# The MLP's token layer norm two groups ahead in a window-attention, MLP and channel-attention kernel: GpSimd's queue for the last slices, joins ahead of gathers

## What is computed

```python
# first block: shifted-window attention and an MLP over tokens (C = 96)
xn = layernorm(x)                                # over channels
x  = shortcut + unshift(window_attention(shift(xn)))
h  = layernorm(x, norm2_g, norm2_b)              # the token layer norm of the MLP
x  = x + (gelu(h @ fc1_w + fc1_b) @ fc2_w + fc2_b)
# second block: channel attention
xn = (x - mean) * rsqrt(var + 1e-5) * ln_g + ln_b     # mean, var over a whole image
Q, K, V = three times: 1x1 grouped convolution, then depthwise 3x3 convolution of xn
attn = softmax(K^T Q / alpha)                    # 8 heads, 12x12
out  = w_f @ (V attn) + b_f + xn
```

## Time and profile before

| | us |
|---|---|
| median of three runs | 526.51 |
| lowest and highest run | 522.05, 529.94 |
| the profiled execution | 523.45 |
| its span on the core | 521.8 |

### The profile page before, as it was taken

The page is one execution under the profiler, slowest core; times in us unless marked ns, Lnnn a source line. Parts: engine busy times, 40 slices in busy tenths (PEclk is TensorE's granted clock), DMA queues, the critical chain, the costliest instruction groups (busy, mean ns, idle before and its releaser), DMA issues.

```text
span 521.8 us, 23235 instructions
## 1 busy us (share of the span) xinstructions
PE 501.1 (96%) x8942; PEld 321.5 (62%) x8942; DVE 367.0 (70%) x1001; ACT 304.6 (58%) x763; POOL 183.0 (35%) x233
## 2 busy tenths in 40 slices
PE   7999999999999999998899999976999999999996
PEld 7777777777777777776565334333555565555553
DVE  2599999999999999998603466624665655656544
ACT  2477778877777887776434667611344444444332
POOL 8544344344434434442460202222223323323300
PEclk8899999999999999999999999995799999999998
DMA  4211101111110111100031142575244444344411
GB/s 80 62 34 31 30 22 44 30 31 31 31 28 22 26 30 30 30 2 3 12 96 33 37 99 63 118 130 138 66 111 119 109 116 115 109 117 115 111 45 31
DMA packets 41175, 32.47 MB, mean 62 GB/s; under 512 B 19240, under 2 KB 36776, under 8 KB 41128
## 3 DMA queue, kind: packets, MB, share of 16 engines
q1 hardware_dynamic: 37544, 26.11, 19.9%
q0 software_dynamic: 3584, 5.72, 5.1%
HBM read 18.36 MB, written 7.13 MB: 49 GB/s over the span
## 4 chain that ended last, share of the span: by engine, by line
PE 43%; DVE 2%; DMA 2%; SPq 2%; issue 1%; ACT 0%; DVEq 0%
PE ps_hidden L1626 18%; PE ps_hidden L1161 6%; PE ps_y L1661 4%; PE ps_y L1172 4%; PE ps_y L1667 4%; PE ps_turn L1642 3%; PE ps_turn L1652 2%; DMA padded_x<-x_pad 1%; PE ps_y L110 1%; SPq L1108 1%; DMA stream<-y_sliced 1%; SPq L1046 1%; PE ps_turn L909 1%; PE ps_turn L916 1%; DVE normed L1327 0%
## 5 line engine op out<-in xcount | busy, mean ns | idle before, releaser
L413 POOL TENSOR_TENSOR scores<-scores,peak 128x768 f32<-128x768 f32 x64 | 94.3, 1474 | 129.9 <-DVE peak L582 129.9
L1626 PE MATMUL ps_hidden<-x_stack,conv_w 40*32 40x256 f32 x3072 | 101.8, 392 | 0.3 <-issue 0.3
L1046 POOL DMA_DIRECT2D x_stack<-padded_x x96 | 52.4, 548 | 127.9 <-PE ps_hidden L1626 77.6
L476 ACT COPY probs_t<-ps_probs 128x768 f32<-128x768 f32 x64 | 51.1, 799 | 40.1 <-PE ps_probs L736 40.1
L1626 PEld LDWEIGHTS ps_hidden<-x_stack,conv_w 40*32 40x32 f32 x3072 | 53.6, 108 | 30.5 <-issue 15.9
L574 DVE TENSOR_TENSOR scores<-ps_scores,bias 128x768 f32<-128x768 f32 x64 | 61.3, 958 | 6.1 <-PE ps_scores L726 4.4
L582 DVE TENSOR_REDUCE peak<-scores 128x12 f32<-128x768 f32 x64 | 61.0, 953 | 2.4
L749 PE MATMUL ps_out<-v_blocks,probs_t 128*64 128x54 f32 x1536 | 57.2, 224 | 1.0 <-ACT out_t L481 0.9
L749 PEld LDWEIGHTS ps_out<-v_blocks,probs_t 128*64 128x64 f32 x1536 | 50.2, 138 | 12.3 <-issue 12.2
L470 ACT ACTIVATE scores<-scores 128x768 f32<-128x768 f32 x64 | 54.2, 847 | 1.5 <-POOL scores L413 1.5
L736 PE MATMUL ps_probs<-ident,scores 128*128 128x128 f32 x384 | 54.3, 277 | 0.0
(11 more groups left out here) (157 smaller groups left out, 831.1 us busy)
## 6 DMA issues: line engine op xcount, KB each, us to landing
x_stack<-padded_x SPq DMA_DIRECT2D x96, 54.0 KB
x_stack<-padded_x POOLq DMA_DIRECT2D x96, 54.0 KB, 2.7
padded_x<-x_pad SPq DMA_DIRECT2D x32, 121.5 KB, 2.5
x_sliced<-stream SPq DMA_DIRECT2D x48, 64.0 KB, 2.0
stream<-y_sliced SPq DMA_DIRECT2D x48, 64.0 KB, 2.1
out<-y_sb SPq DMA_DIRECT2D x32, 96.0 KB, 2.0
x_now<-in_x SPq DMA_DIRECT2D x32, 72.0 KB, 1.8
stream<-in_x SPq DMA_DIRECT2D x32, 72.0 KB, 1.9
```

The source lines that it names most:

```text
L413: nc.gpsimd.tensor_tensor(sc, sc, peak[:, par, p, :].unsqueeze(2).to_broadcast((128, HEADS, WN)), ALU.subtract).then_inc(s["shifted"], 1)
L476: nc.scalar.copy(probs_t[:, :], ps_turned).then_inc(s["turned_copied"], 1)
L1046: engine.dma_start(last.x_stack[64 * half + i * HC:64 * half + (i + 1) * HC, slot, :, :], rows).then_inc(landed[slot], 16)
L1626: mm = nc.tensor.matmul(ps[32 * k:32 * k + 32, r, :], conv_w[rows, kind, j, k, :], grid(x_stack[rows, slot, k, :], PADW)[:, :, j:j + W], s ...
```

## The change

- TensorE turns the tokens of group g+2 during group g (`ahead`), so those of group 2 in group 0 and those of group 3 in group 1; group 2 turns none. In group 0 the first two fills shrink from 15 to 9 matmuls; both turns of chunks 0 and 1 come ahead of the fill. At the end of the first stage 9 more matmuls of a zero constant are issued behind the last slice's transposes.
- ScalarE copies the tokens accordingly, and makes the deviation of group g+2 after the third GELU of group g, where before it came after the second.
- VectorE measures chunks 8 to 11 before it copies `normed` of group 1, and 12 to 15 among the residuals of group 0.
- The slices of group 3 are issued by GpSimd, on its own semaphore, after its scaling and before its gathers. On SP, `join_y(2, 0)` stands ahead of the gathers of images 0 and 1, and `join_y(2, 2)` ahead of the gathers of images 2 and 3.
- `take_moments(2, 0, 4)` becomes `take_moments(2, 0, 8)`, and `measure_images` of step 0 goes.

```diff
+        fill(nc, ps_out[0:C, 0, 0:C], blank[:, :], 9)          # behind turn_first_slice, end of stage 1
...
+    def slice_x(engine, g, landed):
+
+        need(engine, s["mixed_ready"], (g - 1) * SLICES * 2)
+        for c in range(SLICES):
+            for r in range(QUARTERS):
+                at = (g * QUARTERS + r) * CHUNK
+                engine.dma_start(x_sliced[32 * r:32 * r + 32, g % 2, c, :],
+                                 stream[32 * c:32 * c + 32, at:at + CHUNK]).then_inc(landed, 16)
...
-        for g in range(GROUPS - 2):
-            for c in range(SLICES):
-                join_y(g, c)
-            sp.wait_ge(x_in[g % 2], (g // 2 + 1) * PARTS)
-            slice_x(g + 2)
-        join_y(GROUPS - 2, 0)
+        for c in range(SLICES):
+            join_y(0, c)
+        sp.wait_ge(x_in[0], PARTS)
+        slice_x(sp, 2, x_in[0])
+        for c in range(SLICES):
+            join_y(1, c)
         write_padded(sp, last, 0, 0)
         write_padded(sp, last, 1, 1)
+        join_y(2, 0)
         gather_taps(sp, last, 0, 0, 0, 0, last.stacked_sp)
         gather_taps(sp, last, 1, 0, 1, 0, last.stacked_sp)
-        join_y(GROUPS - 2, 1)
+        join_y(2, 1)
         write_padded(sp, last, 2, 2)
         write_padded(sp, last, 3, 3)
+        join_y(2, 2)
         gather_taps(sp, last, 2, 0, 2, 0, last.stacked_sp)
         gather_taps(sp, last, 3, 0, 3, 0, last.stacked_sp)
-        join_y(GROUPS - 2, 2)
...
 # TensorE
-            if g > 1 and r < 2:
-                pe.wait_ge(s["normed_ready"], g * SLICES)
-            if g > 1 and r > 1:
+            if r < 2:
+                pe.wait_ge(s["normed_ready"], (g - 1) * SLICES)
+            else:
                 pe.wait_ge(s["tokens_copied"], k - 1)
...
+            if g + 1 < GROUPS and c < 2:                        # in turn_back
+                pe.wait_ge(s["tokens_copied"], (g + 1) * QUARTERS + 3 + c)
...
             up(g, 0)
+            if ahead:
+                turn_tokens((g + 2) * QUARTERS)
             if g == 0:
-                fill(nc, ps_y[0:C, 0, 0:C], average[:, :], 15)
-            if later:
-                turn_tokens((g + 1) * QUARTERS)
+                turn_tokens((g + 2) * QUARTERS + 1)
+                fill(nc, ps_y[0:C, 0, 0:C], average[:, :], 9)
...
             up(g, 1)
+            if ahead:
+                turn_tokens((g + 2) * QUARTERS + 2)
+                turn_tokens((g + 2) * QUARTERS + 3)
             if g == 0:
-                fill(nc, ps_y[0:C, 0, 0:C], average[:, :], 15)
+                fill(nc, ps_y[0:C, 0, 0:C], average[:, :], 9)
...
 # GpSimd
+        slice_x(pool, GROUPS - 1, x_in_last)
         for t in range(SLOTS):
             gather_taps(pool, last, t, 0, t, 1, last.stacked_pool)
...
 # ScalarE
             gelu(g, 2)
+            if ahead:
+                nc.scalar.preload_act_table_set("natural_log_exp_and_others")
+                token_deviation(nc, act, m, s, g + 2)
+                nc.scalar.preload_act_table_set("gelu_and_others")
...
 # VectorE
+        for k in range(2 * QUARTERS, 3 * QUARTERS):
+            measure(k)
         for c in range(SLICES):
             copy_normed(1, c)
...
-        take_moments(2, 0, 4)
+        take_moments(2, 0, 8)
...
-            for early in range(SLOTS - 1):
+            for early in range(1, SLOTS - 1):
```

More of the change, by code:

```diff
@@ L1082, in mlp @@
     x_in = [sem("x_in0"), sem("x_in1")]
+    x_in_last = sem("x_in_last")
     y_out = last.joined
@@ L1091, in tokens_home @@
         return by_blocks(ps_turn[:, k % 2, :])
-    def run_sp(sp):
-        def slice_x(g):
-            need(sp, s["mixed_ready"], (g - 1) * SLICES * 2)
-            for c in range(SLICES):
[L1098 to L1101, removed]
+    def slice_x(engine, g, landed):
[5 more added lines that the diff above has]
+                                 stream[32 * c:32 * c + 32, at:at + CHUNK]).then_inc(landed, 16)
+    def run_sp(sp):
         def join_y(g, c):
@@ L1109, in join_y @@
                              y_sliced[32 * r:32 * r + 32, g % 2, c, :]).then_inc(y_out[g % 2], 16)
-        slice_x(0)
-        slice_x(1)
+        slice_x(sp, 0, x_in[0])
+        slice_x(sp, 1, x_in[1])
         for half in range(ROUNDS):
@@ L1134, in run_sp @@
         for c in range(SLICES):
-            join_y(GROUPS - 1, c)
+            join_y(3, c)
     def run_pe(pe):
@@ L1184, in run_pe @@
             more = g + 1 < GROUPS
-            later = more and g > 0
+            ahead = g + 2 < GROUPS
             up(g, 0)
+            if ahead:
+                turn_tokens((g + 2) * QUARTERS)
             if g == 0:
-                fill(nc, ps_y[0:C, 0, 0:C], average[:, :], 15)
-            if later:
-                turn_tokens((g + 1) * QUARTERS)
+                turn_tokens((g + 2) * QUARTERS + 1)
+                fill(nc, ps_y[0:C, 0, 0:C], average[:, :], 9)
             if not more:
@@ L1198, in run_pe @@
                 down(g - 1, 0)
-            if later:
-                turn_tokens((g + 1) * QUARTERS + 1)
+            if ahead and g > 0:
+                turn_tokens((g + 2) * QUARTERS + 1)
             up(g, 1)
+            if ahead:
+                turn_tokens((g + 2) * QUARTERS + 2)
+                turn_tokens((g + 2) * QUARTERS + 3)
             if g == 0:
-                fill(nc, ps_y[0:C, 0, 0:C], average[:, :], 15)
-            if later:
-                turn_tokens((g + 1) * QUARTERS + 2)
-                turn_tokens((g + 1) * QUARTERS + 3)
+                fill(nc, ps_y[0:C, 0, 0:C], average[:, :], 9)
             if g > 0:
@@ L1284, in run_act @@
         for g in range(GROUPS):
-            later = 0 < g < GROUPS - 1
+            ahead = g + 2 < GROUPS
             gelu(g, 0)
-            if later:
+            if ahead:
                 for r in range(2):
-                    copy_tokens(nc, act, m, s, (g + 1) * QUARTERS + r, tokens_home(r))
+                    copy_tokens(nc, act, m, s, (g + 2) * QUARTERS + r, tokens_home(r))
             if g + 1 == GROUPS:
@@ L1334, in add_residual @@
             dve.wait_ge(s["y_ready"], n + 1)
-            dve.wait_ge(x_in[par], (g // 2 + 1) * PARTS)
+            if g + 1 < GROUPS:
+                dve.wait_ge(x_in[par], (g // 2 + 1) * PARTS)
+            else:
+                dve.wait_ge(x_in_last, PARTS)
             need(dve, y_out[par], g // 2 * PARTS)
@@ L1360, in run_dve @@
         nc.vector.tensor_scalar(w["taps_b"][:, 1:2], w["taps_b"][:, 1:2], last.recip_alpha[:, 0:1], None, ALU.mult).then_inc(last.taps_scaled, 1)
+        for k in range(2 * QUARTERS, 3 * QUARTERS):
+            measure(k)
         for c in range(SLICES):
             copy_normed(1, c)
-        measure(2 * QUARTERS)
-        measure(2 * QUARTERS + 1)
+        measure(3 * QUARTERS)
         add_residual(0, 0)
-        measure(2 * QUARTERS + 2)
-        measure(2 * QUARTERS + 3)
+        measure(3 * QUARTERS + 1)
+        measure(3 * QUARTERS + 2)
+        measure(3 * QUARTERS + 3)
         add_residual(0, 1)
```

5 lines of the change are left out of this document (removed).

## The result

The changed kernel takes 506.43 us (median of four runs, 504.95 to 508.78) against 524.28 for the kernel before (four runs, 520.97 to 529.94). The ratio is 0.9684, with a 95% interval of 0.9602 to 0.9766: faster by 3.2%, some 12 to 21 us. The ratios here leave disturbed executions out, so they can differ from the quotient of two medians. The profiled execution took 504.95, with a span of 503.3 us.

What follows compares the result with a forecast made beforehand. TensorE, busy 96% of the span, was taken as the bound, losing time to pauses and half clock. Savings 2.9 + 6.86 + 6.32 = 16.1 us from a 526.5 median gave 510.4, rounded to 510, range 504 to 519.

Steps and rivals of the forecast that it cites:

- (1): Barrier before the MLP: opens 0.9 us later, but the clock holds and the first up saves 1.76; net -0.9 us.
- (2): MLP, group 0: smaller fills plus turned chunks stay covered by GELU; two places give -0.26 us, bounds 0 and -0.4.
- (3): MLP, group 2: no tokens turned, up and down back to back, GELU still hides; net -1.77 us.
- (5): MLP to channel attention: joins issued earlier, so TensorE's pause (6.86 us) and the half clock behind it (6.32 us) go.
- group 3's joins: SP's queue: they end at about 348 us instead of 359.4, and step 1's measure_images finds them landed.
- The rule on GpSimd's descriptors: GpSimd's slices: the skill gives some 3100 ns per DMA beside a VectorE copy; twelve would take some 37 us.
- (A): Transition does not close: TensorE still stands 1.5 to 2 us and the clock falls; saved 7.8, time 518.7; chance 0.2.
- (B): GpSimd's slices held up by VectorE, decisive from 1.4 us an issue; time 530; chance 0.05.
- (C): Transition: joins not the true wait, another transfer holds it; only the MLP's 2.9 us saved, 523.6; chance 0.07.

Runs made afterwards that it cites:

- experiment 3: Kernel after without the 9 added matmuls at the barrier ending the first stage: 506.38 us (eight runs).
- experiment 1: Kernel before with only group 3's slices on GpSimd, joins ahead of gathers and eight moments at the end of the MLP: 507.3 us, ratio 0.9737.
- experiment 5: Kernel after with the slices of group 3 back on SP, behind the joins of group 1: 515.09 us, ratio 0.9853.
- experiment 11: Kernel after with 8 more VectorE statistics into a spare tile (2.7 us) ahead of the copy of image 0's tokens: 513.76 us, ratio 0.9872.
- experiment 6: Kernel after with SP's order around group 2 as before, joins behind gathers; slices stay on GpSimd: 515.04 us, ratio 0.9854.
- experiment 4: Kernel before with 36 constant matmuls in TensorE's pause ahead of image 0's 12x12 products: 516.62 us, ratio 0.9868.
- experiment 9: Kernel after with 5 matmuls at the barrier, 3 behind group 0's third up part, and two last-image pauses of stage 1 filled: 504.98 us, ratio 0.9694.
- experiment 7: Kernel after with four images' moments at the end of the MLP and the other four in step 0, as before: 509.6 us, ratio 0.9777.
- experiment 8: Kernel after with 5 matmuls in place of 9 at the barrier and 3 in place of 6 behind group 0's third up part: 505.6 us, ratio 0.9723.
- experiment 12: Kernel before with slices on GpSimd, joins ahead of gathers, eight moments, and stage 1's two last-image pauses filled: 509.16 us, ratio 0.9762.

## Why the prediction was right, point by point

The forecast was 510 us in 504 to 519, from 16.1 us saved; 506.43 was measured, and 17.85 us between the medians. Of the distance of 4.0 us to the unrounded 510.4, 2.2 lie in the kernel before, which was measured at 524.28 in place of 526.51. The mechanism was right. By its steps:

- **(1), the barrier**, net -0.9: in the profiles +0.77 for the later barrier and -1.76 for the clock, -0.99. Right here, but the argument was too sure: experiment 3 and six profiles show that the clock falls there only about half the time. In the mean this step is worth nothing by that count, so that it came out at -0.99 is luck, and leaving it out costs nothing.
- **(2), group 0**: `up` parts 5.39 us apart (255.66 to 261.05), as named (5.4). ScalarE's table loads fitted before the next GELU.
- **(3), group 2**: `up` and `down` back to back, GELU still hidden; the MLP is shorter by 3.91 - 1.76 = 2.15 us besides the clock, and 2.03 were forecast for (2) and (3). 0.14 of it is there without the layer norm part (experiment 1: 84.55 against 86.45 - 1.76).
- **(5), the transition**: the last join of group 2 issued at the moment its data were there and no wait on VectorE, as forecast; the pause went by 5.82 in place of 6.86. The missing 1.0 is the short stall of 0.50 us, and slower matmuls round it, inside image 1's first convolution. The clock stayed: 6.60 against 6.32, because the first of the two steps is 4.62 us and not 4.90. VectorE finished the copy at 342.34 and TensorE took it up at 344.11: 1.8 us to spare, 0.7 were forecast. The surplus is that stall with the slower matmuls round it.
- What the prediction had wrong in (5), though it didn't show in the time, is why slices had to leave SP. It argued with the joins of group 2. Experiment 5 shows that these would land in time anyway; it is group 3's joins, wanted in step 1 by `measure_images`, that need SP free. The prediction had them down in one sentence as harmless.
- **The rule on GpSimd's descriptors.** Twelve issues took 5.98 us (496 to 586 ns each) while VectorE was busy with residuals and normalisation. "SBUF — State Buffer" of the Trainium skill, as cited in the prediction, has some 3100 ns for one beside a copy by VectorE; nothing of that kind was seen with the operations that ran here: by its estimate twelve would have taken 37 us, and those of this tile landed 2.0 to 3.0 us after their issue. The kernel had no SBUF-to-SBUF copy by VectorE in that stretch, so the rule itself was not tested.
- **Rivals.** (A) did not come, but experiment 11 shows it 1.8 us of spare time away and prices a pause of 1.05 us at 5.3 us by stretches, 7.3 by medians. (B) did not come: 0.5 us an issue, where 1.4 were needed. (C) falls with experiments 1 and 6: the joins were the true wait.

The 3.5 us of the first stage in the two profiles are a difference of executions, not of kernels; the median's 17.85 us and its interval cover both 15.0 and 16.1, so no term can be corrected by it.

## What to carry to other kernels

A pause of about a microsecond on TensorE is priced by what its clock does behind it, mostly four to nine microseconds here, so look for the wait that ends it in the queue that issues the transfers, and set transfers with late readers behind those with early ones. When one queue is loaded, ask for every transfer left on it, not for the first late one alone: two joins and two readers stood here, and each half of the remedy alone gave half. When the runs of a kernel lie in heaps, find the short pauses ahead of the stretch where the clock differs, and fill them with constants in a bank that is free; compare traces by stretches, since a median over heaps hides parts of 2 us.

## What the runs showed that was not expected

- **The length of a pause of about one microsecond does not decide whether the clock falls.** Behind 0.93 and 0.62 us, with 0.91 us of work between, it fell in four of eleven profiles; behind 1.41 us in three of six; behind 1.05, 1.31, 1.35 and 0.76 with 0.44 us it fell; behind 0.50, 0.61, 0.92 and 1.47 it held. Behind 0.66 us it held in eight of eight. A fall cost 4.8 us once and 6.4 three times at the last image of the first stage, 1.76 us at the barrier, and in channel attention from 1.6 us (experiment 4) over 4.5 (experiment 11) to about 9 (experiment 6: 23.90 us for three steps, 14.83 in experiment 9).
- **There is a fourth such place, near the kernel's start.** TensorE waits there for its first images. Behind 0.89 us it went on at full speed in the profile of the kernel after. In the other thirteen it waited 0.99 to 1.73 us and ran at half speed behind that (in experiment 3 two matmuls of line 702 take 1.06 us as in the kernel before, against 0.60 in the kernel after, though the clock row says 1.00). By the start of the last image's pause these profiles are 1.6 to 3.7 us later than that of the kernel after. No run fills this pause.
- **A stall that belongs to a place in TensorE's program.** In image 1's first convolution the kernel after pauses before the 26th of 48 matmuls, named "issue": 0.50 us, and 1.47, 0.76, 0.92 and 0.20 us at the same matmul in experiments 5, 6, 7 and 11. In experiment 8, with seven float32 constants fewer (28 instructions with their weight loads), it moved to the 40th matmul, 14 pairs of load and matmul later:

```profile
344.04 0.64 PE L1635 MATMUL ps_hidden<-x_stack,conv_w 40*32 40x256 f32 x9 [0.61 <-issue]
```

That fits a distance from the program's start better than a wait for data. Experiments 1, 9 and 12, with other counts, have no such stall. The view of the transfers bears on it: a queue of the kind "instruction" (q8) moves one packet of 0.02 MB at a time. In the kernel after one starts between 340.25 and 340.50 us, behind the start of the first convolution (338.20), and the stalled matmul starts at 343.11. In experiments 5, 6, 7, 8 and 11 the stalled matmul also starts 2.5 to 2.9 us behind such a packet. In experiment 1 the packet starts by 340.00, over two microseconds ahead of the first convolution (342.53), and in 9 and 12 likewise. That TensorE's instructions arrive late where the stall is fits these rows; no run changes their arrival alone, so it stays open. A smaller pause of this kind (0.29 us at 356.20) is the larger part of the +0.54 us between images 2 and 5.
